# Two-layer recurrent and attention kernel: the transfers that stack the queries' lower halves are begun on the scalar engine's queue instead of SyncE's

## What is computed

```python
x = L0_attn_x
xn = _layernorm(x)
x = x + L0_attn(xn) * silu(L0_experts(xn))      # 2 x 512 tokens, 256 channels
xn = _layernorm(x)
# L1 attention, H=32, KVH=8, HD=64, per batch of 512 tokens
q, k, v = rope(xn @ Wq.T), rope(xn @ Wk.T), xn @ Wv.T
k, v = repeat(k, 4), repeat(v, 4)
attn = softmax(where(causal, q @ k.T / sqrt(64), min))
x = x + ((attn @ v) @ Wo.T) * silu(L1_signed(xn))
```

## Time and profile before

| | us |
|---|---|
| median of three runs | 866.17 |
| the three runs | 873.36, 864.58, 866.17 |
| the profiled execution | 859.47 |
| its span, first to last instruction | 857.7 |

### The profile page before, as it was taken

How to read it: one execution, slowest core, us unless ns; L and a number is a source line. 1 busy time by engine, 2 the same in 40 slices (tenths; PEclk the granted TensorE clock), 3 DMA queues, 4 the chain that set the end, 5 groups by cost and what they waited for, 6 DMA issues and landing times.

```text
span 857.7 us, 13872 instructions
## 1 busy us (share of the span) xinstructions
PE 718.9 (84%) x4504; PEld 624.3 (73%) x4504; DVE 509.6 (59%) x1029; ACT 398.7 (46%) x1017; POOL 415.4 (48%) x463
## 2 busy tenths in 40 slices
PE   1996783678999889905849899999999999999995
PEld 1884563678888888805637788888888888888874
DVE  7797984111312112157477577777777777777764
ACT  3653232211211111122535667777676667767663
POOL 3238882001010010133264777778777777868550
PEclk9999998889999999956968999999999999999999
DMA  9101002978878778332541333322222232212001
GB/s 311 14 1 36 27 38 79 297 284 262 293 232 284 243 254 283 121 104 41 168 133 49 105 78 81 81 62 68 63 67 64 77 81 70 77 47 62 23 1 50
DMA packets 99212, 100.96 MB, mean 118 GB/s; under 512 B 57776, under 2 KB 69360, under 8 KB 99024
## 3 DMA queue, kind: packets, MB, share of 16 engines
q1 hardware_dynamic: 96768, 95.12, 37.2%
q0 software_dynamic: 2384, 5.12, 1.6%
HBM read 69.52 MB, written 13.39 MB: 97 GB/s over the span
## 4 chain that ended last, share of the span: by engine, by line
PE 53%; DVE 18%; issue 10%; ACT 8%; POOL 5%; DMA 3%; SPq 2%; POOLq 0%; DVEq 0%; ACTq 0%
PE bank L1464 14%; PE bank L1483 7%; PE bank L1317 7%; PE bank L1321 5%; PE bank L1322 5%; PE bank L1323 5%; ACT prob L1108 3%; PE bank L1560 3%; DVE nmax L868 3%; POOL prob L1279 2%; DVE xs L704 2%; PE bank L1561 2%; ACT kv_hi L1115 2%; DVE gate L750 1%; SPq L462 1%
## 5 line engine op out<-in xcount | busy, mean ns | idle before, releaser
L1279 POOL TENSOR_TENSOR prob<-prob,rinv 128x128 f32<-128x128 f32 (+3 forms) x256 | 178.0, 727 | 105.9 <-DVE rinv L873 105.9
L1108 ACT ACTIVATE prob<-bank,nmax 128x512 f32<-128x512 f32 (+3 forms) x256 | 133.3, 529 | 53.8 <-DVE nmax L868 53.5
L877 DVE TENSOR_TENSOR kv_lo<-bank,kv_hi 128x512 fp32r<-128x512 f32 x160 | 110.0, 687 | 49.1 <-ACT kv_hi L1115 48.2
L1464 PE MATMUL bank<-xgT,wm 128*128 128x128 f32 x920 | 112.2, 283 | 23.4 <-issue 16.3
L1115 ACT ACTIVATE kv_hi<-bank 128x512 fp32r<-128x512 f32 x160 | 96.3, 602 | 72.2 <-PE bank L1317 71.3
L1464 PEld LDWEIGHTS bank<-xgT,wm 128*128 128x128 f32 x920 | 109.3, 199 | 26.1 <-issue 17.8
L1242 POOL DMA_INDIRECT y_rows<-y_row,to_row x23 | 22.2, 966 | 195.0 <-DVE y_row L777 173.6
L868 DVE TENSOR_REDUCE nmax<-bank 128x1 f32<-128x512 f32 (+2 forms) x192 | 91.1, 502 | 18.1 <-PE bank L1563 18.1
L1317 PE MATMUL bank<-cst,prob 128*128 128x128 f32 x640 | 98.7, 278 | 2.4 <-ACT prob L1108 1.2
L1560 PE MATMUL bank<-kT,qT 128*128 128x512 f32 (+3 forms) x256 | 83.8, 333 | 19.1 <-ACT prob L1108 17.9
L1321 PE MATMUL bank<-kv_hi,v_lo 128*128 128x128 f32 (+3 forms) x256 | 92.8, 363 | 0.3 <-DVE kv_lo L877 0.3
(11 more groups left out here) (273 smaller groups left out, 1507.2 us busy)
## 6 DMA issues: line engine op xcount, KB each, us to landing
wm<-in_w_moe SPq DMA_DIRECT2D x23, 1920.0 KB, 7.8
qT<-q_hi SPq DMA_DIRECT2D x128, 64.0 KB, 2.0
qT<-q_lo SPq DMA_DIRECT2D x128, 64.0 KB, 2.0
k_exp<-k_rows SPq DMA_DIRECT2D x56, 64.0 KB, 2.0
x_sorted<-zeros SPq DMA_DIRECT2D x1, 2944.0 KB, 12.1
wtl<-in_w_moe_tail SPq DMA_DIRECT2D x46, 64.0 KB, 7.3
xg<-x_sorted SPq DMA_DIRECT2D x1, 2432.0 KB, 15.9
gy<-y_rows SPq DMA_DIRECT2D x8, 256.0 KB, 4.6
```

The lines of the kernel that those rows point to most:

```text
L1108: ins = actv(prob[:, i % 2, h, POFF[j]:POFF[j] + (j + 1) * P], bk[:, at:at + (j + 1) * P], ACT.Exp, bias=nmax[:, i % 2, h, j:j + 1], accum ...
L1279: ins = GT(seg, seg, rinv[:, i % 2, k, j:j + 1].to_broadcast([P, (j + 1) * P]), ALU.mult)
L1464: ins = mm(dst, w(c), xgT[:, u, c, :], start=c == 0, stop=c == KC - 1)
```

## The change

The eight transfers of a half that read `q_lo` go from `move_q` on SP to a new `move_lower_q` on ACT. In the list it is the entry `"m"` at step n+6 with priority 9, so it follows ACT's `E` of that step and precedes ACT's `T` of the next one. For the very first half it is called directly, after `upper_k(0, 0)` and before the last five `copy_v`. It waits for both `l` instructions of its half (`qlo_done`) and, from the third half on, for the scores that last read this buffer (`score_full`). The transfers, their sizes, their count and the semaphore that they add to stay the same.

```diff
     def half(i, n, slow):
         z = [(n, 8, "Q", i, 0), ... (n + 3, 6, "a", i, 0),
-             (n + 4, 6, "a", i, 1), (n + 5, 8, "h", i, 0)]
+             (n + 4, 6, "a", i, 1), (n + 5, 8, "h", i, 0), (n + 6, 9, "m", i, 0)]
         return z + [(n + 6, 6, "l", i, 0), (n + 6 + slow, 6, "l", i, 1)]
...
             def move_q(g, b):
                 hh = g * 2 + b
-                for src, done in ((q_hi, qhi_done), (q_lo, qlo_done)):
-                    at = 0 if src is q_hi else 2
-                    sp.wait_ge(done, hh + 1 if at == 0 else hh * 2 + 2)
-                    if at == 0 and g > 0:
-                        sp.wait_ge(score_full, g * STEPS + (b * 10 + 10 - STEPS))
-                    for i in range(2):
-                        for h in range(GQ):
-                            sp.dma_start(qT[(at + i) * 32:(at + i + 1) * 32, b, h, :].bitcast(F32),
-                                         src[h * 32:(h + 1) * 32, i, :].bitcast(F32)).then_inc(q_in[b], 16)
+                sp.wait_ge(qhi_done, hh + 1)
+                if g > 0:
+                    sp.wait_ge(score_full, g * STEPS + (b * 10 + 10 - STEPS))
+                for i in range(2):
+                    for h in range(GQ):
+                        sp.dma_start(qT[i * 32:(i + 1) * 32, b, h, :].bitcast(F32),
+                                     q_hi[h * 32:(h + 1) * 32, i, :].bitcast(F32)).then_inc(q_in[b], 16)
...
+            def move_lower_q(now, i):
+                hh = now * 2 + i
+                act.wait_ge(qlo_done, hh * 2 + 2)
+                if i > 1 or not isinstance(now, int):
+                    act.wait_ge(score_full, now * STEPS + (i * 10 + 10 - STEPS))
+                for s in range(2):
+                    for h in range(GQ):
+                        act.dma_start(qT[(2 + s) * 32:(3 + s) * 32, i % 2, h, :].bitcast(F32),
+                                      q_lo[h * 32:(h + 1) * 32, s, :].bitcast(F32)).then_inc(q_in[i % 2], 16)
...
+                    elif op == "m":
+                        move_lower_q(now, i)
...
             copy_v(2)
             upper_k(0, 0)
+            move_lower_q(0, 0)
             for t in range(3, NT):
                 copy_v(t)
```

## The result

The changed kernel takes 969.65 us (median, 966.65 to 973.63) against 867.86 us for the kernel before run beside it. The ratio is 1.117, with a 95% interval from 1.109 to 1.124. The profiled execution has a span of 971.8 us and a mean granted clock of 0.905.

The account below looks back on a forecast made before the run. PE was taken to bound the kernel, busy 24.33 of 24.5 us per half. Idle PE of 73.9 us plus 30.8 us lost to the clock made 104.7 us, taking the median from 866.17 to 970.9 us, range 928 to 1005.

Parts of the forecast that it names:

- type A: First coming half of a group: PE idles 5.1 us in each of the six middle groups, 30.6 us together.
- type B: Second coming half of a group: PE idles 5.5 us each time, 4.9 in the last half.
- third half: In the first group: the rotation PE waits for starts at 484.6 instead of 478.07, 6.6 us of idle PE.
- second half: Lower transfers just behind an exponential ACT had waited for: 0.5 us of idle PE, between 0 and 2.
- start of the stage: First half: SP saves issuing time, so ACT's split of the values comes 1.7 us earlier, a gain.
- clock, fourteen stalls: After each stall PE runs 4.4 us at half clock, losing 2.2 us, 30.8 us over fourteen stalls.
- The price of an issue: Each transfer begun on ACT occupies its queue 0.63 us, eight 5.0 us, as the same transfers did on SP.
- second rival: Beginning a transfer on ACT is as cheap as SP's cheapest, 0.4 us, eight 3.2 us: 935 us; chance 0.12.
- third rival: Issues cost ACT nothing, only the wait for POOL is left, about 3 us: 869 us, within 1%; chance 0.06.
- first rival: The clock holds through the stalls, DVE's order adding some 0.5 us a stall: 947 us; chance 0.15.
- Dearer on ACT: Rival: issues on ACT take 1.0 us each, blocks 3 us longer: 1021 us; chance 0.10.
- faster: Rival: SP is free 5 us earlier each half, key and value loads land sooner, over 1% faster; chance 0.02.

Follow-up runs that it names:

- it stands alone: Against the kernel before, only the very first half's eight lower transfers are begun by ACT, SP keeping the rest: 864.10 us, ratio 1.000.
- four: Changed kernel with only four of each half's eight lower transfers on ACT, the other four back on SP: 925.41 us, ratio 1.069 to the kernel before.
- sixteen: Changed kernel with ACT also beginning the upper eight transfers of each half, SP none: 1064.23 us, ratio 1.228 to the kernel before.
- the kernel that only waits: Changed kernel with ACT's waits kept in place but all sixteen transfers of a half begun by SP: 887.59 us, ratio 1.024 to the kernel before.
- with the gaps filled: Changed kernel with zero-matrix matmuls keeping PE busy before the scores that stall: 961.33 us; without the last group's 21 needless ones 955.58 us, ratio 1.106.
- pairs: Changed kernel with ACT's eight issues spread two at a time over four steps: 872.20 us, ratio 1.007 to the kernel before.
- singles: Changed kernel with ACT's eight issues spread one at a time over eight steps: 865.00 us, ratio 1.001 to the kernel before.

## Why the prediction held, and where its terms were off

The median was forecast as 970.9 us and is 969.65. The terms, against the trace:

| term of the sum | forecast, us | in the trace, us |
|---|---|---|
| type A, six | 5.1 each | 4.96 to 5.19 |
| type B, three in the middle and one in the first group | 5.5 each | 5.61 to 5.66 |
| type B at a loop's turn, two | 5.5 each | 8.49 and 8.57 |
| type B, last | 4.9 | 5.54 |
| third half | 6.6 | 5.9 (one gap of 9.11 for 1.46 and 1.80) |
| second half | 0.5 | 1.6 |
| start of the stage | -1.7 | -2.1 in PE's wait, of which nothing is left at the end when it stands alone |
| idle time of PE together | 73.9 | 80.5 |
| clock, fourteen stalls | 2.2 each, 30.8 | 1.5 to 3.1, mean 2.1, 30.0; about 2 less than that is new, as the third half and the two before it had half clock already |

The idle time and the clock's loss of the trace come to about 108 us, and the stage is 106.1 us longer. So adding the two, as the prediction did, gives the length of this kernel to some 2 us. Where those 2 us go was not traced; 0.7 of them are small waits for POOL and DVE in the steady stretch that are there before and not after.

*Which engine bounds.* Right. PE had no slack in the steady stretch and every stall is in the span.

*The price of an issue.* Right, and it was the choice that mattered. It was not seen on ACT before, and taking the rows of the same transfers on SP (590 ns) rather than the cheapest issue nearby gave the 612 ns that came. The second rival, 0.4 us an issue, falls with this row and with the type A stalls for four, eight and sixteen.

*Behind the block.* Right: ACT's next activation follows the last issue at once, and PE's stalls are one piece each. The Trainium skill's page "Perfetto Trace Analysis", section "DMA Instruction — HWDGE (DVE, Sync)", says that the sequencer stays occupied until the descriptors are made, and the trace agrees for ACT, with 5.0 us for eight. The third rival (issues free on ACT) was also priced too low: it gave 869 us for the wait alone, and the kernel that only waits takes 887.6. That rival and with it the word "small" of the Trainium skill's "DMA: Bandwidth & Descriptors", section "Issuing engines are not separate DMA queues", do not hold for eight in a row. For single issues laid beside activations they do.

*The loop's turn.* Missed, 6 us. The end of that block in the changed kernel's chain of waits:

```profile
641.98 0.05 ACTq L1185
642.03 2.67 issue
644.70 0.07 ACTq L1185
```

In this view `issue` is time for which the profile shows no wait. L1185 is ACT's loop over groups. Between its last issue and the next group's first activation ACT's queue stood 2.7 us behind the loop's branch. Before the change the branch took as long (2.6 us, 589.15 to 591.78), but most of it lay beside activations that ACT had in hand, and 1.13 us of idle time in the row of `wq_hi` was all that showed; PE did not feel it.

The turn isn't always as long. The same place with four issues on ACT:

```profile
621.55 0.05 ACTq L1190
621.61 0.21 issue
621.82 0.07 ACTq L1190
```

It took 2.4 to 2.8 us in ten of the twelve kernels here and 0.2 us, both times, in two: with four issues, and with the block two steps later. That the issues lie behind the turn doesn't decide it, since those of the pairs and singles do too and it took 2.4 to 2.6 us there, while with four they lie ahead of it. What decides it was not tested. It matters to the comparisons: these two kernels were spared some 2.3 us of ACT's queue at each turn that the others had.

*The clock.* The length at half clock was right (4.4 us forecast, 3.0 to 6.3 found after resuming), and the first rival, that it holds, is wrong. The clock's part of the sum was right too, 30.8 us forecast and 30.0 found. What this does not say is what a steady clock would give back: with the gaps filled it was 1.1 to 1.3 us a stall, not 2.2, as PE then waits for the others instead. There the first rival's own price failed. It allowed 0.5 us of such waits per stall and no loop's turn, and gave 947 us; the runs show 0.8 and the turn, and 955.6 us.

*How much was luck.* The parts that missed cancel. Idle time was forecast 6.6 us too low, nearly all of it the loop's turn; the clock's loss was forecast about 3 us above what is new of it, and some 2 us of the two together don't show in the length. (By its own figures the third half is 484.6 - 478.07 = 6.5 and not 6.6 us, which changes nothing.) The change in the medians is 101.8 us for a forecast of 104.7, and that the two absolute times agree within 1.3 us also owes something to the kernel before, whose median was 866.17 in the table and 867.86 in the result.

*Dearer on ACT, faster.* Neither came: single issues of up to 1.65 us occur, but fifteen of the sixteen blocks take 5.0 to 5.5 us, and the one of the second half 6.05.

## What to carry to other kernels

A queue with idle time is not a free place for transfers: each issue here took 0.6 us of it, and what counts is the longest absence that the engine behind it can bear, not the share of busy time. ACT had 7 us free in 24.5, and a block of 8 us cost PE 5 to 5.6, while the same eight issues laid one by one beside its activations left the time where it was (ratio 1.001, 0.997 to 1.004). To price such a move, find the first instruction of the bounding engine that needs what stands behind the block, and take its start in the trace of before from the time at which it can now start. The difference is the stall.

## What was not expected of the hardware

- ACT's queue can begin a transfer while ACT computes: in the kernel with singles an issue at 585.30 lies beside an activation at 585.33. With the block two steps later the first issues lie beside activations too, and ACT idles 4.2 us of a block of 5.
- Coming back to the head of a loop took ACT's queue 2.6 to 2.7 us in the changed kernel (once from 642.03 to 644.70), both times that it came back, and 2.4 to 2.6 us before, hidden there. With waits alone in the same place, PE's stall there was 4.2 us against 0.6 elsewhere. In two kernels it took 0.2 us, for a reason that no run shows.
- A stall of 2.4 us may or may not cost clock. With four issues PE came back at 537.39 after 2.41 us and kept full clock up to its next stall, came back at 565.65 after 3.07 us and ran at half clock from 567 to 570.4. The next stall of 2.40 us, ended at 594.34, was followed by half clock too. Windows of that kernel:

```profile
537.40:565.60 28.20, 24.65 (x154) 20.95 (x154) 18.27 (x38) 17.63 (x50) 19.70 (x23) 1.00 0.27 66
567.00:568.00 1.00, 1.00 (x7) 0.90 (x5) 1.00 (x2) 0.99 (x5) 1.00 (x2) 0.51 0.00 0
...
570.00:571.00 1.00, 1.00 (x6) 0.85 (x5) 0.22 (x1) 1.00 (x3) 0.00 (x0) 0.79 0.05 16
```

  In the changed kernel half clock followed every one of the fourteen stalls, until 3.0 to 6.3 us after PE resumed. Why a stall of 2.4 us does so in one place and not in another was not looked into.
